# A decoder layer on one core: the projections of its first attention as three float32r passes over split operands

## The reference

```python
q = _heads(x @ Wq); k = _heads(x @ Wk); v = _heads(x @ Wv)      # 256 -> 16 heads x 64
qf = _feature_map(q, Kq)                                        # softmax(q Kq), softmax(-q Kq)
kf = _feature_map(k, Kk)
kv = jnp.cumsum(kf[:, :, :, None, :] * v[..., None], axis=2)    # causal state
o = jnp.einsum('bhlf,bhldf->bhld', qf, kv) / z[..., None]       # z: the same with kf alone
return y @ Wo                                                   # y: o with the heads joined
```

## Time and profile before

| | |
|---|---|
| Three timed runs | 1217.22, 1218.51, 1218.55 us; median 1218.51 |
| Profiled execution, first to last instruction | 1218.4 us |
| Granted TensorE clock, mean | 0.986 of full |
| PE busy | 1139.0 us (93%) |
| DVE busy | 954.2 us (78%) |
| ACT busy | 612.3 us (50%) |
| POOL busy | 371.0 us (30%) |

### The profile page before, as it was taken

One profiled execution on the slowest core, in us unless ns is written; L12 is line 12 of the kernel. 1 busy time (PEld: TensorE's weight loads), 2 busy tenths in 40 slices (PEclk: granted clock), 3 DMA queues, 4 the chain that ended last, 5 costly groups with the idle time before them and its releaser, 6 DMA issues. The chain is left out here.

```text
span 1218.4 us, 29643 instructions
## 1 busy us (share of the span) xinstructions
PE 1139.0 (93%) x11668; PEld 685.0 (56%) x11669; DVE 954.2 (78%) x1745; ACT 612.3 (50%) x1166; POOL 371.0 (30%) x351
## 2 busy tenths in 40 slices
PE   7899899999999999879999999999999847999996
PEld 6566666676677777643443344334434334676665
DVE  5989968987888688788778778877889466677757
ACT  4332333334333333227777767777788722344443
POOL 2422255222522222113200320221100424556651
PEclk9899999999999999999999999999999978999999
DMA  7100026000400000025720580075050152121125
GB/s 242 48 1 2 2 51 111 2 2 1 82 1 2 1 2 2 1 59 83 151 35 9 105 157 2 8 141 95 2 212 2 53 139 93 61 65 61 63 60 210
DMA packets 62200, 73.64 MB, mean 60 GB/s; under 512 B 14352, under 2 KB 53392, under 8 KB 61440
## 3 DMA queue, kind: packets, MB, share of 16 engines
q1 hardware_dynamic: 58288, 61.56, 21.3%
q0 software_dynamic: 3792, 10.36, 2.8%
HBM read 52.86 MB, written 18.78 MB: 59 GB/s over the span
## 5 line engine op out<-in xcount | busy, mean ns | idle before, releaser
L1737 DVE TENSOR_REDUCE neg_max<-pS 128x1 f32<-128x1024 f32 x238 | 285.0, 1220 | 50.9 <-PE pS L1520 50.8
L1652 ACT ACTIVATE pt<-pR 128x512 f32<-128x512 f32 x512 | 286.3, 600 | 73.4 <-PE pR L1543 68.5
L1543 PE MATMUL pR<-qs,ks 100*32 100x512 bf16 x2048 | 192.4, 381 | 1.9 <-ACT pt L1652 1.6
L1520 PE MATMUL pS<-ks,qs 100*32 100x512 bf16 x1904 | 146.4, 378 | 3.4 <-DVE neg_max L1737 1.8
L1557 PE MATMUL b_pO<-pt,b_v 128*32 128x512 f32 x1024 | 135.0, 598 | 3.0 <-ACT pt L1652 2.3
L411 PE MATMUL pP<-w_feat,a_xT 128*128 128x512 f32 x244 | 116.4, 600 | 0.7 <-ACT w_feat L689 0.7
L1543 PEld LDWEIGHTS pR<-qs,ks 100*32 100x32 bf16 x2048 | 57.2, 96 | 93.7 <-issue 23.8
L301 POOL TENSOR_TENSOR kf<-kf,fsum 128x2048 f32<-128x2048 f32 (+1 forms) x17 | 58.1, 3420 | 163.8 <-DVE fsum L883 163.8
L301 POOL TENSOR_TENSOR qs<-qs,fsum 128x2048 f32<-128x2048 f32 (+1 forms) x17 | 58.5, 3446 | 141.2 <-DVE fsum L883 141.2
L716 ACT COPY qfT<-pT 128x512 f32<-128x512 f32 x64 | 37.2, 582 | 126.3 <-PE pT L439 126.3
L1399 POOL COPY qs<-max_rows 3x512 bf16<-3x512 bf16 x60 | 36.7, 611 | 210.1 <-ACT max_rows L1645 207.1
(11 more groups left out here) (353 smaller groups left out, 2145.0 us busy)
## 6 DMA issues: line engine op xcount, KB each, us to landing
ks<-k_scr SPq DMA_DIRECT2D x8, 768.0 KB
qs<-q_scr SPq DMA_DIRECT2D x24, 256.0 KB
k_scr<-f SPq DMA_DIRECT2D x18, 256.0 KB, 2.7
ks<-k_scr SPq DMA_DIRECT2D x8, 512.0 KB
ks<-in_L_ffn_w_dram SPq DMA_DIRECT2D x2, 2048.0 KB, 10.5
ks<-in_L_ffn_w_dram SPq DMA_DIRECT2D x4, 1024.0 KB, 9.2
ks<-y_rows SPq DMA_DIRECT2D x16, 256.0 KB, 5.3
cx<-in_ctx_dram SPq DMA_DIRECT2D x3, 768.0 KB, 12.4
```

Of the source, the lines that this page charges most:

```text
L1520: ins = pe.matmul(pS1[q:q + XV, slot, 512 * half:512 * half + 512], qs[0:KR, bass.ds(par, 1), h, P * t + q:P * t + q + XV].rearrange("r a ...
L1543: ins = pe.matmul(ring[bank][q:q + XV, :], ks[0:KR, bass.ds(par, 1), h, P * j + q:P * j + q + XV].rearrange("r a n -> r (a n)"), qs[0:KR, ...
L1652: nc.scalar.activation(pt[:, j % 2, i, :], ring[bank], ACT.Exp).then_inc(exp_done, 1)
L1737: nc.vector.tensor_reduce(neg_max[:, hg % 2, u // G, u % G:u % G + 1], pS1[:, u % 2, :], AX_X, ALU.max, negate=True).then_inc(max_done, 1)
```

## The change

Each operand of the three projections is split into a part rounded to float32r (`w_hi`, `xT_hi`) and the rest (`w_lo`, `xT_lo`, float32r too), and a half projection becomes three products for each of its two steps, all float32r: hi by lo, hi by hi, lo by hi. That is six float32r matmuls of 512 columns for two fp32 ones.

ACT's copies now write the rounded parts. Eight new VectorE instructions (`w_rest(r)`, 128x512) and one for each tile (`x_rest(t)`, 128x256) subtract them from what is still in PSUM. GpSimd splits Wv after its load, in four instructions of 128x1024, ahead of its scaling. The waits follow: the projections wait for `w_split`, `wv_split` and `xT_split` in place of `w_cp`, `s_wv` and `xT_ready`. In the tiles `x_rest(t + 2)` stands in VectorE's queue behind the update of the fourth group and ahead of its `normalise_o`. The low parts and the raw Wv lie in `ks[:, 0]`; so only heads 0 to 3 of the first keys are loaded where all 16 were, and the other twelve when the last v projection is done (`v_proj` at 2T), and token score unit 16 waits for them. SP clears the stage's semaphores at the head of the cross attention.

```diff
-        w_feat = sb("w_feat", [P, 2, KD, H * HD])
-        wv = sb("wv", [P, KD, H * HD])
+        w_hi = sb("w_hi", [P, 3, KD, H * HD], F32R)
+        w_lo = [late_keys("wk_lo", [P, KD, H * HD], 8), late_keys("wq_lo", [P, KD, H * HD], 12),
+                late_keys("wv_lo", [P, KD, H * HD], 4)]
+        wv_raw = ks[:, 0, 0:4].rearrange("p h n -> p (h n)").bitcast(F32).rearrange("p (k n) -> p k n", k=KD)
...
-                sp.dma_start(ks[AUG:KR, 0], aug_scr[0].unsqueeze(1).broadcast_to([4, XH, M])).then_inc(first_loaded, 16)
+                sp.dma_start(ks[AUG:KR, 0, 0:G], aug_scr[0].unsqueeze(1).broadcast_to([4, G, M])).then_inc(first_loaded, 16)
...
+                sp.wait_ge(v_proj, 2 * T)
+                sp.dma_start(ks[AUG:KR, 0, G:XH], aug_scr[0].unsqueeze(1).broadcast_to([4, XH - G, M])
+                             ).then_inc(rest_loaded, 16)
+                for at, n in K_RUNS:
+                    sp.dma_start(ks[XD * at:XD * (at + n), 0, G:XH],
+                                 k_scr[0, 0:n].rearrange("c (d h) n -> (c d) h n", d=XD)[:, G:XH]
+                                 ).then_inc(rest_loaded, 16)
...
+                pool.wait_ge(s_wv, 16)
+                for half_of in range(2):
+                    cols = slice(512 * half_of, 512 * half_of + 512)
+                    nc.gpsimd.tensor_copy(w_hi[:, 2, :, cols], wv_raw[:, :, cols]).then_inc(wv_split, 1)
+                    pool.wait_ge(wv_split, 2 * half_of + 1)
+                    nc.gpsimd.tensor_tensor(w_lo[2][:, :, cols], wv_raw[:, :, cols], w_hi[:, 2, :, cols].bitcast(F32),
+                                            ALU.subtract).then_inc(wv_split, 1)
...
-                        wait(pe, w_cp, r - 1)
+                        wait(pe, w_split, r - 1)
...
-                def project(w, half, par, done, out=None):
+                def project(m, half, par, done, out=None):
+                    out = pP[:, 512 * half:512 * half + 512] if out is None else out
+                    cols = slice(512 * half, 512 * half + 512)
                     for k in range(KD):
-                        ins = pe.matmul(pP[:, 512 * half:512 * half + 512] if out is None else out, xT[:, par, k, :],
-                                        w[:, k, 512 * half:512 * half + 512],
-                                        start=(k == 0), stop=(k == KD - 1))
+                        pe.matmul(out, xT_hi[:, par, k, :], w_lo[m][:, k, cols], start=(k == 0), stop=False)
+                        pe.matmul(out, xT_hi[:, par, k, :], w_hi[:, m, k, cols], start=False, stop=False)
+                    for k in range(KD):
+                        ins = pe.matmul(out, xT_lo[:, par, k, :], w_hi[:, m, k, cols],
+                                        start=False, stop=(k == KD - 1))
                     ins.then_inc(done, 1)
...
                 def first_k(half):
-                    pe.wait_ge(xT_ready, 1)
-                    pe.wait_ge(w_cp, 2 * half + 2)
+                    pe.wait_ge(xT_split, 1)
+                    pe.wait_ge(w_split, 2 * half + 2)
...
+                def w_rest(r):
+
+                    wait(dve, w_cp, r + 1)
+                    m, col = r // 4, 2 * P * (r % 4)
+                    heads = (slice(None), slice(None), slice(col, col + 2 * P))
+                    nc.vector.tensor_tensor(
+                        w_lo[m][heads].rearrange("p k (j n) -> p j k n", j=2),
+                        pP[:, 512 * (r % 2):512 * (r % 2) + 512].rearrange("p (j k n) -> p j k n", j=2, k=KD),
+                        w_hi[:, m][heads].bitcast(F32).rearrange("p k (j n) -> p j k n", j=2),
+                        ALU.subtract).then_inc(w_split, 1)
+
+                def x_rest(t, par):
+
+                    wait(dve, xT_ready, t + 1)
+                    nc.vector.tensor_tensor(xT_lo[:, par], x_ps.rearrange("p (k n) -> p k n", k=KD),
+                                            xT_hi[:, par].bitcast(F32), ALU.subtract).then_inc(xT_split, 1)
...
                 normalise(0)
+                w_rest(1)
+                x_rest(0, 0)
                 statistics(1)
+                w_rest(2)
                 statistics(2)
...
                 shift(0, 0, 0, 0, own)
+                w_rest(3)
                 shift(0, 0, 1, 0, own)
+                w_rest(4)
                 statistics(3)
+                w_rest(5)
                 variances(TB, T)
                 denominators(0, 0, 0, own, HALVES[0], 0)
+                w_rest(6)
                 normalise(1)
+                w_rest(7)
                 denominators(0, 0, 0, own, HALVES[1], 1)
                 shift(1, 0, 0, 0, own)
+                x_rest(1, 1)
                 shift(1, 0, 1, 0, own)
...
                             if c < TB - 1:
                                 update(b, c, g)
+                            if g == G - 1 and has2:
+                                x_rest(t + 2, par)
                             normalise_o(t, g, own)
```

More of the change, by code:

```diff
@@ L12 @@
 F32 = mybir.dt.float32
+F32R = mybir.dt.float32r
 BF16 = mybir.dt.bfloat16
@@ L261, in _ @@
                     for at, n in K_RUNS:
-                        sp.dma_start(ks[XD * at:XD * (at + n), 0, :, now],
-                                     k_scr[0, 0:n].rearrange("c (d h) n -> (c d) h n", d=XD)[:, :, now]
+                        sp.dma_start(ks[XD * at:XD * (at + n), 0, 0:G, now],
+                                     k_scr[0, 0:n].rearrange("c (d h) n -> (c d) h n", d=XD)[:, 0:G, now]
                                      ).then_inc(first_loaded, 16)
@@ L489, in out_product @@
                     wait(pe, oT_ready, 2 * t + 2)
-                    wait(pe, xT_ready, xT_count)
+                    wait(pe, xT_split, xT_count)
                     wait(pe, x1_done, t)
@@ L544, in token_scores @@
                         pe.wait_ge(v_copied, 2 * T)
+                    elif u == NEW:
+                        pe.wait_ge(rest_loaded, 16 * (len(K_RUNS) + 1))
                     elif u == SOON:
@@ L607, in _ @@
                 first_v(1)
-                wait(pe, xT_ready, 2)
+                wait(pe, xT_split, 2)
                 wait(pe, v_copied, 1)
-                project(w_feat[:, 0], 0, 1, proj[0])
+                project(0, 0, 1, proj[0])
                 wait(pe, shifted[1], 2)
-                project(w_feat[:, 0], 1, 1, proj[0])
+                project(0, 1, 1, proj[0])
                 transposes(0, 0, 0)
@@ L696, in x_copy @@
                     wait(act, v_proj, 2 * (t - 1))
-                    nc.scalar.copy(xT[:, par], x_ps.rearrange("p (k n) -> p k n", k=KD)).then_inc(xT_ready, 1)
+                    nc.scalar.copy(xT_hi[:, par], x_ps.rearrange("p (k n) -> p k n", k=KD)).then_inc(xT_ready, 1)
                 def exponentials(m, t, half, par):
@@ L839, in variances @@
                     nc.vector.tensor_scalar(rstd[:, a:z], mv[:, a:z, 1], LN_EPS, None, ALU.add).then_inc(s_var, 1)
+                def w_rest(r):
[11 more added lines that the diff above has]
+                                            xT_hi[:, par].bitcast(F32), ALU.subtract).then_inc(xT_split, 1)
+                w_rest(0)
                 statistics(0, range(1))
@@ L1082, in _ @@
                 batch(B - 1, True)
+    return range(min(s.num for s in held), max(s.num for s in held) + 1)
 CD = 192
@@ L1321, in store_q @@
                     wait(sp, stored[2], 48 * b)
+                sp.sem_clear(done_sems)
                 for w, src in ((wq_raw, Wq), (wo, Wo)):
@@ L2596, in decoder_layer @@
             "p (g j c) -> p g j c", g=G, j=JT)
-        linear_attention(nc, x, a_wq, a_wk, a_wv, a_wo, a_kq, a_kk, xr, ctx_in, mask, x_wq, x_wk,
-                         x_wv, k_scr, q_scr, aug_scr, stats, mv, rstd, q_scale, q_aug, neg_max, ks, qs, v_first)
+        done_sems = linear_attention(nc, x, a_wq, a_wk, a_wv, a_wo, a_kq, a_kk, xr, ctx_in, mask, x_wq, x_wk,
+                         x_wv, k_scr, q_scr, aug_scr, stats, mv, rstd, q_scale, q_aug, neg_max, ks, qs, v_first, ks_at)
         w1_sb = ks[:, 0].rearrange("p h n -> p (h n)").bitcast(F32).rearrange("p (e k h) -> p e k h", e=E_, k=KD)
```

44 lines of the change are left out of this document (26 added, 18 removed).

## The result

The changed kernel takes 1233.99 us in the median of four runs (1229.25 to 1236.27); the kernel before 1218.05 (1217.22 to 1218.55). The ratio is 1.0115 [1.0091, 1.0138], some 16 us slower, where 6.3 were forecast. The profiled execution is the fastest of the four: 1229.25 us, span 1227.0, 8.6 above the span of 1218.4.

What follows compares the result with a forecast made beforehand. VectorE's queue, not TensorE, was taken to bound the first attention. From 1218.4 us, the start added 7.9 and the tiles took off 1.5, giving 1224.8 us, 0.5% slower; range 1206 to 1236.

Steps and rivals of the forecast that it cites:

- What bounds it: First attention: VectorE's queue is a closed chain around the tile; TensorE is late by only 0.2 to 0.3 us.
- Price of a pass: Projections: a float32r pass of 512 columns takes 0.216 us, six 1.30, so a half gains 0.42 us.
- (a) to (d): First attention's tiles: x_rest costs VectorE time, tiles 3, 7 and 11 gain; sum -1.5 us, bounds -5 to +3.
- The wait before `project_k`: Tiles: TensorE waits about 0.95 us before project_k(t + 2, 0), covered by 0.3 us, so no cost.
- the one before the state: Tiles: VectorE's wait for the state falls to near 1.3 us in place of 1.50.
- (c): Tiles 1, 2, 5 and 0, 4, 8, 12: x_rest costs +0.35 us each, +2.5 together; tile 14 -0.2.
- (e) to (h): Start, before tile 0: w_rest, x_rest(1) and waits for ScalarE delay it 6.7 to 9.0 us, taken as 7.9.
- The other stages keep their code and start later as a whole.: All stages behind the first attention: unchanged code, only shifted in time, no cost of their own.
- The rivals: TensorE bound, 1188 us, 7%; part comes back, 1208, 14%; cheap start, 1220, 14%; slow passes, 10%; late keys, 1235, 2%.
- Slow passes: Projections: a pass takes 0.43 us, about 1290 us; or weight loads no longer hide, about 1236; together 10%.

Runs made afterwards that it cites:

- the second one: The changed kernel, unchanged, run again for a second trace: 1231.07 us, 1.0099 of the kernel before.
- the paced one: Changed kernel with SyncE waiting for each load of queries and keys in the cross attention before issuing the next: 1263.24 us, 1.0352.
- the early kernel: Changed kernel with x_rest(t + 2) behind the third group's normalise_o (c below 3), w_rest(3) ahead of the first shift, statistics(2) and x_rest(1) later: 1225.16 us, 1.0039.
- The fill: Changed kernel with nine transposes in each TensorE wait before project_k(t + 2, 0) and 66 small ones at the start: 1231.55 us, 1.0095.

## Why the prediction was wrong

**What bounds it: right.** TensorE isn't the bound. With two matmuls for a half in place of six the kernel is no faster than with four.

**Price of a pass: right.** 0.23 us, taken 0.216. A half gains 0.32 us, not 0.42, which is why tiles 3, 7 and 11 give less than forecast.

**(a) to (d), tiles: right in the first trace, -1.75 against -1.5, and in part by luck.** `x_rest` costs 0.1 to 0.3 in the tiles 1 to 13 with c below 3; tiles 3, 7 and 11 give 1.35, 1.07 and 1.09, together 0.8 less than forecast, and tile 0, booked at +0.35, came out at -0.4. In the two other traces with the same code up to here, the second one and the paced one, the tiles cost 0.3 and 0.4 us, since each has half clocks at 237 and 326 us. The forecast had counted TensorE's clock in the start alone. The wait before `project_k` is 0.92 (0.95), the one before the state 1.36 (1.3). (c) was wrong in one point: it said that tiles 0, 4, 8 and 12 have no wait worth having. The waits at L952 (3.6 us in 4 times) are theirs, and the early kernel hid `x_rest` in them. The trace of before had shown the same waits:

```profile
DVE state L902 <- PE pO L474: 3.6, 4, 0.9
```

**(e) to (h), start: right, when traces at the same clock are compared.** Forecast +7.9, from a sum of 6.7 to 9.0; five traces with this start gave +4.85, +6.00, +6.35, +7.8 and +8.1. It goes by the clock: full between 12 and 25 us in the first, halved once in the next two (near 21.8), twice in the last two (near 13 and 23). From the first to the last that is 6.8 us more at half clock for 3.3 us. The Trainium skill ("TensorE: Matmul & The Clock Gate", Terms) puts the penalty at the throttled time times one minus the ratio, half of it here; these two traces agree. The trace that I counted from has a half clock at 13.1 itself. The kernel before with 192 transposes, the same code up to here, has none, and its rows are the ones to hold against the first trace of the changed kernel: first shift +0.8 (16.94), forecast +0.6; denominators of q +6.8 (39.59).

```profile
16.14 0.69 DVE L868 TENSOR_REDUCE hi<-pO 128x8 f32<-128x512 f32 x1 [0.96 <-PE pO L411]
...
32.79 1.21 DVE L882 TENSOR_REDUCE fsum<-qs 128x16 f32<-128x1024 f32 x1
```

**The failed step: "The other stages keep their code and start later as a whole."** Set at 0, it measured +5.5 us in the first trace and +2.3 in the second, from TensorE's late fetches and, in the first, two half clocks, one behind the first wait and one at 547 us. These are differences to a trace of before without such a wait; the second trace of before has one and +3.8 itself, so the medians tell the price better: 384 instructions more cost the kernel before 6 us, and moving the fetches or the loads gives the early kernel 4. The step counted DMAs, semaphores and engine time of the change, but not its instructions. The change makes TensorE's stream 384 longer, the fetches of every later stage move against its loads, and they hit the query bursts of the cross attention.

**A base that was off.** I took the profiled execution as 0.1 us from the median, since its span was. Nearly all runs lie 1.7 to 1.9 above their span (the profiled one of the changed kernel 2.25), so the trace of before comes from an execution of about 1220.1, 1.6 above the median of 1218.51.

**What stays open.** The first trace accounts for 4.85 - 1.75 + 5.5 = 8.6 of the 16 us. Some 2 are the base that was off, 0.5 the larger gap between time and span, and 4.7 lie between the profiled run and the median, in timed runs without a trace. Their mean clock is 0.975 to 0.979 against 0.982; from 0.982 to 0.975 is 17 us more at half clock, for 7.5 us of span. Where these fall wasn't seen, apart from the places in the second trace (22, 237, 326 us). The fill, which took those in the tiles away, didn't bring the time back.

**The rivals.** None of them was this one. "Slow passes" had about the right time (1236) for a wrong reason, which the spacing of 0.23 us excludes.

## What to carry to other kernels

A change that lengthens one engine's instruction stream moves its instruction fetches in all later code. Look in the trace for waits of kind "issue" and for the instruction queue's transfers beside bursts of loads, and break a burst that fills all DMA engines for 12 us with one wait; here that gave 4 and 9 us in the two kernels where it was tried, whose traces without it show the late fetches. A wait before every load cost some 30. Put a new VectorE instruction where VectorE waits, not where its operand is next needed: the same `x_rest` cost nothing one place earlier. Of the kernels run, only the one with a single product and no split, which drops the low parts, beats the kernel before (0.9921); with all three products the best is level (1.0004).

## What the runs showed of the hardware

In the cross attention a fetch of 16 KB behind a burst of loads (12 us on all DMA engines around 690 us) began with up to 511 matmuls and weight loads started since the last. At 472 and more TensorE then stood 1.1 to 2.5 us each time (twelve cases), at 468 0.5 to 0.6 (three), at 460 0.2. Waits of 0.6 to 1.3 also came at distances of only 364 to 444 (seven cases), and others of this size had none; so the distance alone doesn't tell the whole. The Trainium skill ("Runtime: NRT & Kernel Launch", Instruction fetch mechanics) calls crossing a 16 KiB boundary mostly hidden. Most fetches here agree: of the 91 in the changed kernel's first trace, two have a wait of over 1 us behind them in the cross attention. These two don't.

Relieving TensorE cost clock. The changed kernel had 0 and 2 spells of half clock in the tiles, the one with four products 7, the one with two 14; the two spells of the changed kernel's second trace cost 1.4 and 1.2 us. A transpose of 32x32 costs 0.032 to 0.036 us (64 in 2.04, 192 in 6.84).
